# A graph layer and a routed feed-forward on one core: the gathered edge rows are weighted, and split into two float32r parts, on VectorE in lots of four

## The reference, cut to what matters

```python
# x (12500, 256), src/dst (200000,) with dst sorted, edge_weight (200000,)
def _L0_gnn_ref(X, edge_src, edge_dst, edge_val, W, b):
    support = X @ W
    msgs = support[edge_src] * edge_val[:, None]
    out = jax.ops.segment_sum(msgs, edge_dst, num_segments=N_NODES)
    return out + b
def _L0_ffn_ref(x, Wr, br, W1, b1, W2, b2, gamma, beta):     # E = 8 experts, D = 256, F = 512
    logits = jnp.mean(x, axis=1) @ Wr + br                   # one routing for all rows
    ...                                                      # the two largest experts, two weights
    h = jax.nn.gelu(jnp.einsum('nd,edf->enf', xf, W1) + b1[:, None, :], approximate=False)
    y = jnp.einsum('enf,efd->end', h, W2) + b2[:, None, :]
    out = jnp.einsum('ne,end->nd', w_dense, y).reshape(B, S, D)
    return _layer_norm(out + x, gamma, beta)
x = x + _L0_gnn_ref(_layernorm(x), src, dst, edge_weight, W, b)
x = x + _L0_ffn_ref(_layernorm(x)[None], ...)[0]
```

## Time and profile before

| | |
|---|---|
| median of three executions | 2384.93 us |
| the profiled execution | 2382.08 us, its span 2380.3 us |
| TensorE busy (mean granted clock) | 2210.0 us, 93% (0.985) |
| GpSimd busy | 1516.3 us, 64% |
| ScalarE busy | 1193.3 us, 50% |
| VectorE busy | 1025.3 us, 43% |
| first gather to last gather | 11.27 to 1974.58 us |

### The profile page before, as it was taken

How to read it: one execution, slowest core, us unless ns; L and a number is a source line. 1 busy time by engine, 2 the same in 40 slices (tenths; PEclk the granted TensorE clock), 3 DMA queues, 4 the chain that set the end, 5 groups by cost and what they waited for, 6 DMA issues and landing times. The chain is left out here.

```text
span 2380.3 us, 41661 instructions
## 1 busy us (share of the span) xinstructions
PE 2210.0 (93%) x9949; PEld 1729.8 (73%) x9950; DVE 1025.3 (43%) x2952; ACT 1193.3 (50%) x3202; POOL 1516.3 (64%) x1594
## 2 busy tenths in 40 slices
PE   2488999899999999999999999999998999999998
PEld 1366777677776767777777777777776777999998
DVE  7893233232332233232332322232222235899989
ACT  3577666665655555544534343322324125565664
POOL 6777777777777777777777777777777771000100
PEclk9999999999999999999999999999999999999999
DMA  9955667666666655566656656556566554242431
GB/s 369 336 168 157 205 202 241 187 189 180 180 187 181 181 176 175 178 179 197 186 178 180 189 179 187 175 182 190 169 194 172 186 161 141 95 140 95 136 98 54
DMA packets 226740, 425.79 MB, mean 179 GB/s; under 512 B 36675, under 2 KB 134774, under 8 KB 226600
## 3 DMA queue, kind: packets, MB, share of 16 engines
q0 software_dynamic: 75008, 204.90, 29.5%
q1 hardware_dynamic: 151160, 217.12, 28.0%
q10 hardware_dynamic: 432, 2.40, 0.3%
HBM read 341.53 MB, written 82.75 MB: 178 GB/s over the span
## 5 line engine op out<-in xcount | busy, mean ns | idle before, releaser
L588 POOL DMA_INDIRECT G<-xr_d,SRC x1467 | 1391.8, 949 | 447.0 <-issue 298.6
L1072 DVE TENSOR_SCALAR OH<-CST,DL,WR 128x128 f32<-128x128 f32 x1563 | 567.4, 370 | 1272.3 <-PE ps L1463 1151.0
L1463 PE MATMUL ps<-G,OH 128*128 x3126 | 739.8, 389 | 78.6 <-DVE OH L1072 57.8
L1463 PEld LDWEIGHTS ps<-G,OH 128*128 128x128 f32 x3126 | 597.0, 194 | 224.1 <-issue 143.0
L1446 PE MATMUL ps<-W2u,H 128*128 128x256 f32 x1920 | 430.9, 382 | 6.9 <-issue 6.3
L1435 PE MATMUL ps<-YU,W1u 128*128 128x512 f32 (+1 forms) x1024 | 426.1, 568 | 9.6 <-ACT H L767 8.4
L1446 PEld LDWEIGHTS ps<-W2u,H 128*128 128x128 f32 x1920 | 363.1, 191 | 69.8 <-issue 20.9
L1435 PEld LDWEIGHTS ps<-YU,W1u 128*128 128x128 f32 x1024 | 194.8, 191 | 206.1 <-issue 184.7
L775 ACT ACTIVATE YE<-ps 128x512 f32<-128x512 f32 (+1 forms) x128 | 72.6, 569 | 442.3 <-PE ps L1446 442.1
L767 ACT ACTIVATE H<-ps,b1a 128x512 f32<-128x512 f32 (+1 forms) x256 | 168.5, 660 | 225.9 <-PE ps L1435 225.6
L602 POOL TENSOR_TENSOR ZR<-ZV,mhalf 128x4 f32<-128x4 f32 (+1 forms) x24 | 30.5, 1272 | 348.6 <-DVE ZV L1256 348.6
(11 more groups left out here) (221 smaller groups left out, 2302.1 us busy)
## 6 DMA issues: line engine op xcount, KB each, us to landing
W1u<-in_W SPq DMA_DIRECT2D x64, 512.0 KB
W2u<-in_W SPq DMA_DIRECT2D x64, 512.0 KB, 4.7
y_d<-YE SPq DMA_DIRECT2D x56, 512.0 KB, 5.7
G<-xr_d,SRC POOLq DMA_INDIRECT x1467
x_d<-X SPq DMA_DIRECT2D x98, 128.0 KB
yt_d<-YT SPq DMA_DIRECT2D x98, 128.0 KB
XR<-in_x SPq DMA_DIRECT2D x97, 128.0 KB, 3.1
XL<-x_d SPq DMA_DIRECT2D x24, 512.0 KB, 4.9
```

Source lines behind the costliest of these rows:

```text
L588: e.indirect_dma_start(out=G[0:rows(s), held(s), :], out_offset=None, in_=x if s < FRESH else xr_d, in_offset=bass.IndirectOffsetOnAxis(ap ...
L1072: e.tensor_scalar(OH[:, s % OHR, :], iota, DL[:, s:s + 1], WR[:, s + 1:s + 2], ALU.is_equal, ALU.mult).then_inc(s_oh, 1)
L1463: e.matmul(ps[:, 0, 0:D], OH[:, r, :], Gf[:, bass.ds(g + r * D, D)], start=False, stop=True, skip_group_check=True).then_inc(s_main, 1)
```

## The change

1. `one_hot` is taken apart. From slot 96 on, VectorE works in lots of four (`LOT`) in `parts`: it multiplies the four gathered rows in place by their weights (128x1024), makes four matrices of 0 and 1 in one comparison (128x512, `one_hots`), copies the product rounded to float32r (`GW[.., 0, ..]`), and subtracts to get the low part (`GW[.., 1, ..]`). Fresh slots get one multiply of 128x256 each (`weighted`) and a comparison for four. The last three slots have their own `last_parts`.
2. `edge` becomes two float32r products for slots from 96 on (line 1504 of the changed kernel), one float32 product for the others (line 1501). `begin` takes up the last four slots in place of two.
3. `G` has 36 places in place of 72, and gathers wait once for each lot, for VectorE's last reading of the place (`s_gw`), not for TensorE. `OH` and the new `GW` have 16 places.
4. ScalarE makes four columns of `OHX` in `match`; `copy` no longer waits for TensorE's products nor multiplies by weights.
5. The first group has 4 tiles, so 32 in place of 30 tiles are done ahead, 64 full units. The group of two tiles is now the second of the last stage, which has 66 tiles. `room` is weighed anew.

```diff
-RING, GS, OHR = 64, 16, 8
+HELD, GS, LOT, RING = 36, 9, 4, 16
+OWN, TURN = 8, NE - 44
-HELD = RING + OHR
...
-SMALL = 2
-NG = (NT - SMALL + GT - 1) // GT + 1
 AHEAD = 8
+SMALL = NT - AHEAD * GT - (NT - AHEAD * GT) // GT * GT
+SIZES = [GT] * (AHEAD + 1) + [SMALL] + [GT] * ((NT - AHEAD * GT) // GT - 1)
...
+def before(s):
+    return s - (HELD if s < TURN + HELD - OWN else HELD - OWN)
...
-    room = [max(0.0, 0.75 * slots[t] - 3.5) * most[t] if t >= 14 else 0.0 for t in range(NT)]
+    room = [max(0.0, slots[t] - 4.5) * most[t] if t >= 12 else 0.0 for t in range(NT)]
...
             for s in range(NE):
-                if s >= HELD:
-                    e.wait_ge(s_main, s - RING + 3)
...
-                if s >= GS:
-                    e.wait_ge(gat[s % GS], 16 * (s // GS))
+                if s >= HELD and s % LOT == 0:
+                    e.wait_ge(s_gw, before(s) + LOT)
+                if s >= GS * LOT and s % LOT == 0:
+                    e.wait_ge(gat[s // LOT % GS], 16 * LOT * (s // (LOT * GS)))
...
-            def one_hot(s):
-                if s < FRESH:
-                    e.wait_ge(s_pow, STEPS * (batch_of[s] + 1))
-                elif rows(s):
-                    e.wait_ge(gat[s % GS], 16 * (s // GS + 1))
+            def one_hots(s, m):
...
-                if s >= OHR:
-                    e.wait_ge(s_main, s - OHR + 1)
-                e.tensor_scalar(OH[:, s % OHR, :], iota, DL[:, s:s + 1], WR[:, s + 1:s + 2], ALU.is_equal, ALU.mult).then_inc(s_oh, 1)
+                if s >= RING:
+                    e.wait_ge(s_main, s - RING + m + 1)
+                e.tensor_tensor(out=OH[:, s % RING:s % RING + m, :], in0=iota.unsqueeze(1).to_broadcast([P, m, P]),
+                                in1=DL[:, s:s + m].unsqueeze(2).to_broadcast([P, m, P]), op=ALU.is_equal).then_inc(s_oh, m)
+
+            def weighted(s):
+                if s % LOT == 0:
+                    one_hots(s, LOT)
...
+                e.tensor_scalar(GF[:, s % RING, 0, :], G[:, held(s), :], WR[:, s + 1:s + 2], None, ALU.mult).then_inc(s_gw, 1)
+
+            def parts(s):
+                g, r = slice(held(s), held(s) + LOT), slice(s % RING, s % RING + LOT)
+                e.wait_ge(gat[s // LOT % GS], 16 * LOT * (s // (LOT * GS) + 1))
+                e.tensor_tensor(out=G[:, g, :], in0=G[:, g, :], in1=WR[:, s + 1:s + LOT + 1].unsqueeze(2).to_broadcast([P, LOT, D]), op=ALU.mult).then_inc(s_gm, 1)
+                one_hots(s, LOT)
+                e.wait_ge(s_gm, (s - FRESH) // LOT + 1)
+                e.tensor_copy(GW[:, r, 0, :], G[:, g, :]).then_inc(s_gh, 1)
+                e.wait_ge(s_oh, s + LOT)
+                e.wait_ge(s_gh, (s - FRESH) // LOT + 1)
+                e.tensor_tensor(out=GW[:, r, 1, :], in0=G[:, g, :], in1=GW[:, r, 0, :].bitcast(f32), op=ALU.subtract).then_inc(s_gw, LOT)
...
                 if s >= 20:
-                    one_hot(s - 12)
+                    weighted(s - 12)
...
-            def edge(g, r):
-                e.matmul(ps[:, 0, 0:D], OH[:, r, :], Gf[:, bass.ds(g + r * D, D)], start=False, stop=True, skip_group_check=True).then_inc(s_main, 1)
+            def edge(r, fresh):
+                if fresh:
+                    ins = e.matmul(ps[:, 0, 0:D], OH[:, r, :].bitcast(f32), GF[:, r, 0, :], start=False, stop=True, skip_group_check=True)
+                else:
+                    for h in range(2):
+                        ins = e.matmul(ps[:, 0, 0:D], OH[:, r, :], GW[:, r, h, :], start=False, stop=True, skip_group_check=True)
+                ins.then_inc(s_main, 1)
```

More of the change, by code:

```diff
@@ L23 @@
 XG = (NT + GT - 1) // GT
-SMALL = 2
-NG = (NT - SMALL + GT - 1) // GT + 1
 AHEAD = 8
+SMALL = NT - AHEAD * GT - (NT - AHEAD * GT) // GT * GT
+SIZES = [GT] * (AHEAD + 1) + [SMALL] + [GT] * ((NT - AHEAD * GT) // GT - 1)
+STARTS = [sum(SIZES[:g]) for g in range(len(SIZES))]
+NG = len(SIZES)
 UNITS = AHEAD * E
@@ L43, in group, with place_in @@
 def group(t):
-    return 0 if t < SMALL else (t - SMALL) // GT + 1
+    return max(g for g in range(NG) if STARTS[g] <= t)
 def tiles(g):
-    a = SMALL + (g - 1) * GT
-    return range(a, min(a + GT, NT)) if g else range(SMALL)
+    return range(STARTS[g], STARTS[g] + SIZES[g])
+def place_in(t):
+    return t - STARTS[group(t)]
 def part(t):
-    return slice((t - SMALL) % GT, (t - SMALL) % GT + 1)
-def place_in(t):
-    return t - tiles(group(t))[0]
+    return slice(place_in(t), place_in(t) + 1)
 def slot(t):
@@ L87, in events @@
     most = [0.75 if t == NT - 1 else 1.0 for t in range(NT)]
-    room = [max(0.0, 0.75 * slots[t] - 3.5) * most[t] if t >= 14 else 0.0 for t in range(NT)]
-    size = [len(tiles(k // E)) / GT for k in range(UNITS)] + [1.0]
+    room = [max(0.0, slots[t] - 4.5) * most[t] if t >= 12 else 0.0 for t in range(NT)]
     free, u, out = 0.0, 0, []
     for t in range(NT):
-        free += room[t] * sum(size) / sum(room)
+        free += room[t] * (UNITS + 1) / sum(room)
         n = 0
-        while u + n <= UNITS and (free >= size[u + n] / 2 or t == NT - 1):
-            free -= size[u + n]
+        while u + n <= UNITS and (free >= 0.5 or t == NT - 1):
+            free -= 1.0
             n += 1
@@ L110 @@
 assert 2 * NEV <= 512
-assert NE % OHR == 4 and EDGES <= (NE - 1) * P
+assert NE % RING == 12 and FRESH % RING == 0 and EDGES <= (NE - 1) * P
+assert TURN % HELD == OWN and all(held(s) == held(before(s)) for s in range(HELD, NE))
 def gnn_ffn(nc, x, dflat, srct, dstt, wt, W, b, Wr, br, W1, b1t, W2, b2, gamma, beta, cst, iota_e, evt, out):
@@ L1104, in _ @@
                 newton_steps(FRESH // 8 - 1, range(4 * j, 4 * j + 4))
-                one_hot(FRESH - 12 + j)
-            for s in range(FRESH - 8, NE - 1):
-                one_hot(s)
+                weighted(FRESH - 12 + j)
+            for s in range(FRESH - 8, FRESH):
+                weighted(s)
+            for s in range(FRESH, NE - LOT, LOT):
+                parts(s)
+            for s in range(NE - LOT, NE - 1):
+                last_parts(s)
             rn = 0
@@ L1469, in following, with event @@
                 e.reg_mov(rel, e.snap(due) - a)
-            def event(a, r, g):
+            def event(a, r, fresh):
                 with e.While(lambda: e.snap(rel) <= r):
@@ L1487, in event, with slots @@
                         with e.If(now == END):
-                            begin(e.snap(v_r, min_val=1, max_val=FINAL), g + (r - 1) * D)
-            def slots(a, g, n):
-                for r in range(n):
-                    if r % 4 == 0:
-                        e.wait_ge(s_oh, a + (r + 4))
-                    edge(g, r)
-                    if r % 2 == 1:
-                        event(a, r, g)
-            with e.Fori(0, NE // OHR) as i:
-                a = e.snap(i * OHR)
-                g = e.snap(lap_r, min_val=0, max_val=RING * D)
-                e.reg_mov(rel, e.snap(due) - a)
-                slots(a, g, OHR)
-                e.reg_mov(lap_r, (e.snap(lap_r, min_val=0, max_val=RING * D) & (RING * D - 1)) + OHR * D)
+                            begin(e.snap(v_r, min_val=1, max_val=FINAL), r, fresh)
+            def slots(first, last, fresh):
+                with e.Fori(first // RING, last // RING) as i:
+                    a = e.snap(i * RING)
+                    e.reg_mov(rel, e.snap(due) - a)
+                    for r in range(RING):
+                        if r % LOT == 0:
+                            e.wait_ge(s_gw, a + (r + LOT))
+                        edge(r, fresh)
+                        if r % LOT == LOT - 1:
+                            event(a, r, fresh)
+            slots(0, FRESH, True)
+            slots(FRESH, NE // RING * RING, False)
             def last_across():
```

141 lines of the change are left out of this document (78 added, 63 removed).

## The result

The changed kernel took 2589.22 us (median of 3 runs, 2586.89 to 2592.59) for 2384.93: 1.0857 times the time of before, with a 95% interval of 1.0833 to 1.0882. I had forecast 2900, in a range of 2396 to 3010.

What follows compares the result with a forecast made beforehand. The prediction took GpSimd's unbroken chain of gathers, 1.253 us a step, to bound the kernel. Its terms summed as 2382 + 31 - 11 + 499 + 1 = 2902 us, stated as 2900, range 2396 to 3010.

Steps and rivals of the forecast that it cites:

- Start: First slots: with 36 places in G, gathers from slot 36 on wait for VectorE; +31 us, not won back.
- TensorE's part at nothing: Before the last gather: cheaper edge products leave TensorE some 295 us less to do, behind GpSimd's chain; 0 us.
- Last stage: After the edges: 66 tiles in place of 68; -11 us.
- the +1 of the last slot: End of the edges: two more instructions for the last slot, 0.35 and 0.48 us; +1 us.
- The pause: GpSimd between gathers: 0.30 us a step, claimed not to be a wait and to stay.
- the faster rival: Gathers: the pause shrinks as only every fourth slot waits; 275 us less, 2128 us in all; chance 0.04.
- VectorE's load: VectorE from slot 96: a lot takes 3.8 us (3.7 to 4.3) against 5.01 for four gathers, so it keeps up.
- The kinds that hold at the early point: Gathers 0.13 us in: all four kinds of a lot's VectorE instructions stop them until they end; chance 0.56.
- The rival with the copy alone: Gathers from slot 96: only the copy stops them; +133 us, 2535 us in all (2470 to 2540); chance 0.18.
- The late point: Near a gather's end: it waits only for one-input double-rate instructions, here the copy; 0.49 / (8T) us a gather.
- if gathers start at any phase of a lot: Gathers from slot 96: each waits on average for the rest of the running VectorE instruction; +499 us over 1467 gathers.
- average hold of 0.34 us a gather: Gathers from slot 96: pace T rises from 1.253 to 1.59 us; over 1467 gathers +499 us.

Runs made afterwards that it cites:

- 1082 ns beside two inputs: Kernel before plus an unused two-input 128x1024 VectorE sum every fourth slot from 96 on: 3099.18 us, 0.9596 of before on that chip.
- the comparison first: Changed kernel with each lot's comparison put ahead of the wait for gathers and the multiply: 2893.75 and 2900.16 us, 0.896 and 0.8914 of before on their chips.
- the first expectation above on the order: Expectation for the first run with the comparison ahead of the multiply in the changed kernel: 2750 to 2950 us; it took 2893.75 us.
- the reduction of the same shape: One-input VectorE reduction put in place of the copy in the changed kernel; with only the copy replaced: 3034.84, 3047.26 and 3038.8 us.
- the kernel with one-input instructions: Changed kernel with multiply, copy and subtraction replaced by one-input reductions over 1024 columns: 3311.33 us here, 1.0179 of before; 2431.38 us on another chip.
- the one-input control: Kernel before plus an unused one-input 128x1024 VectorE maximum every fourth slot from 96 on: 3234.14 us, 1.0022 of before on its chip.

## Why the prediction was right and wrong

- **Start.** +31 forecast, +29.9 measured; slot 36 at 84.33 us for 86, slot 40 at 89.40 for 91, slot 44 at 99.89 for 101. The steps held one by one.
- **TensorE's part at nothing.** It waited 335.1 us for VectorE and GpSimd's pace was its own; right in the changed kernel. Its sizes were not. I forecast TensorE under 70% busy before the last gather, and it was 81.5% (1703 of 2089.5 us). Two products took 0.341 us a slot (499.7 us for 1467) for 0.235, at a mean granted clock of 0.89 for 0.98: eight of them took 2.07 us at a granted clock of 0.50, behind a wait of 5.58 us (at 1497.61), 0.26 us each, for the 0.1175 that I had read in the last stage. No gather waited for it.
- **Last stage.** -11 forecast, -9.1 measured, and ahead of it +3.8 for the +1 of the last slot: TensorE had waited 3.06 us for VectorE and did its last edges from 2188.9 to 2192.7 us at a granted clock of 0.50, the lower of its two levels (14 products of 256 columns in 3.74 us), where before it stood at 1.00 from 1975 to 1990 us.
- **The pause.** It stayed at 0.30 us, though three gathers of four have no wait: the faster rival is out.
- **VectorE's load.** 1225, 688, 801 and 1225 ns for 1195, 685, 700 and 1195: 3.8 us a lot, as forecast.
- **The kinds that hold at the early point.** All four did. The rival with the copy alone forecast 1.04 us and 2535; the multiply and the subtraction made 130 of the 173 us, so it is out. The Trainium skill's rule ("SBUF — State Buffer", section "Who interferes with whom"), which says that a VectorE instruction with two SBUF inputs blocks a GpSimd one that reads SBUF, stands by these rows: 1082 ns beside two inputs, 958 beside one.
- **The late point did not extend a gather.** In the changed kernel 323 gathers ended 0.3 us into a copy, and those copies took 0.82 us; 40 copies with the end 0.9 us away took 0.69. It was the copy that gave way, by 0.13 us. The prediction had 0.49 of its 4.31 us² from this.
- **The step that failed: "if gathers start at any phase of a lot", and with it the average hold of 0.34 us a gather.** With the true lengths that average is (1.225² + 0.688² + 0.801² + 1.225²) / (8 x 1.378) = 0.37 us a gather; 0.127 were lost. The phases are not free: each lot's start is tied to the landing of its gathers, mostly 1.8 to 1.9 us after the last one's end, and with these lengths the gathers' early points fall near the ends of the instructions, three times of four. In place of +499 us it made +182.6. With the comparison first the same average, 0.32 at its pace of 1.564 us, would have been nearly right: 0.29 us a gather measured, on a slow chip. So the average was the right middle for an unknown order and the wrong value for this one, and the order was known. The early point and most of the lengths were in the earlier trace rows; the delay of a landing was the number to look up. Stepping the rule through the lots gave 1.34 us a slot, in the first expectation above on the order, for the 1.378 measured. It hangs on the delay: by an estimate from the traced lengths, with one fixed delay in place of the real ones, it is 1.28 us a slot at 1.75 us, 1.37 at 2.1, and 1.44 at 1.7. So even with the delay known this step could not have been told to better than some 0.1 us a slot.

## What to carry to other kernels

Where two engines meet at a shared resource and one waits for the other, don't average over phases: lay one period of both out by their durations and the delay between them, and see which points coincide. Beside indirect gathers, prefer VectorE instructions with one SBUF input, or short ones; but one input is not enough by itself, since the copy has one, does 1024 columns in 0.7 to 0.8 us, and held 303 gathers, while the reduction of the same shape in 1.21 us held none. The order within a lot gave mean gathers of 1183 and 1237 ns on one chip. And an engine with a chain without slack makes savings elsewhere worth nothing and small holds worth everything.

## What I had not expected of the hardware

On the slow chips the order of kernels turned round: the freer the gathers, the longer the time. The kernels with mean gathers of 958 to 966 ns took 3234 to 3331 us, with 1082 ns 3099, with 1114 ns 3035 to 3047, with 1183 ns 2986 to 2994, with 1212 and 1237 ns 2819 to 2900. They differ in more than their gathers, so this is an order and not a cause. The changed kernel is 8 to 9% faster than before there, and 9% slower where before takes 2385. What the trace shows is TensorE late with matmuls issued. In the kernel with one-input instructions (3311 us), TensorE, then ScalarE, and the clock by stretches:

```profile
1502.86 7.07 PE L1491 MATMUL ps<-W2u,H 128*128 128x256 f32 x32
1509.77 3.60 PE L1480 MATMUL ps<-YU,W1u 128*128 128x512 f32 x8
1524.84 2.08 PE L1480 MATMUL ps<-YU,W1u 128*128 128x512 f32 x2 [11.47 <-ACT H L772]
```

```profile
1504.97 0.72 ACT L656 ACTIVATE OHX<-OHT,ones 128x512 fp32r<-128x512 f32 x1
1515.74 0.60 ACT L780 ACTIVATE YE<-ps 128x512 f32<-128x512 f32 x1 [10.05 <-remote]
1523.61 0.60 ACT L780 ACTIVATE YE<-ps 128x512 f32<-128x512 f32 x1 [7.27 <-remote]
```

```profile
1512.00:1514.00 2.00, 1.37 (x4) 0.30 (x2) 1.42 (x2) 0.00 (x0) 1.51 (x2) 1.00 0.33 86
1518.00:1520.00 2.00, 0.00 (x0) 0.00 (x0) 0.00 (x0) 0.00 (x0) 1.39 (x3) 0.50 0.27 80
```

ScalarE needs the two halves of the W2 products, which the records end at 1506.5 and 1509.9 us, and gets them at 1515.7 and 1523.6. TensorE's records start nothing from 1512.8 to 1524.8, and the granted clock is still 2.4 GHz then and falls to 1.2 GHz behind, not ahead. The ends of matmuls are modelled, so whether TensorE stood still or ran slowly in between isn't shown. The gathers' DMA packets took as long as in the kernel before on the first chip (22.0% of 3242.7 us in the one-input control and 29.5% of 2380.3 us, 713 and 702 us), and so did those of the other transfers (20.7% and 28.0%, 671 and 666 us), so slow transfers don't explain it. Why two groups of chips differ so, and whether dense work on TensorE brings the stops about, stays open: no run here took the density alone apart.
